# Dense experts of a two-layer decoder: products from coarse and fine operand parts, down products between up products

## The reference, cut to what matters

```
x_attn = _layernorm(x_flat, ln_g, ln_b) @ attn_w + attn_b + x_flat
g = x_attn.reshape(MICRO_BATCHES, E, tpe, Dx)           # 2 x 8 x 128 x 256
h = gelu(einsum('metd,edf->metf', g, w1) + b1)           # w1: 8 x 256 x 1024
y = einsum('metf,efd->metd', h, w2) + b2                 # w2: 8 x 1024 x 256
out = gelu(y @ next_w + next_b)                          # next_w: 256 x 256
x = _layernorm(x + out)                                  # the layer's end
```

## Time and profile before

| what | us |
|---|---|
| median of three runs (lowest, highest) | 2448.28 (2446.01, 2457.68) |
| span of the profiled execution | 2451.3 |
| PE busy | 2287.7 (93%) |
| DVE busy | 1509.6 (62%) |
| ACT busy | 1106.9 (45%) |
| POOL busy | 1062.9 (43%) |
| scatters (L353), 256: busy, and POOL's idle time before them | 416.9, 400.8 |
| first instruction of stage f, of stage d (PE) | 1569.28, 1741.41 |

### The profile page before, as it was taken

One profiled execution on the slowest core, in us unless ns is written; L12 is line 12 of the kernel. 1 busy time (PEld: TensorE's weight loads), 2 busy tenths in 40 slices (PEclk: granted clock), 3 DMA queues, 4 the chain that ended last, 5 costly groups with the idle time before them and its releaser, 6 DMA issues.

```text
span 2451.3 us, 34108 instructions
## 1 busy us (share of the span) xinstructions
PE 2287.7 (93%) x12918; PEld 1434.3 (59%) x12918; DVE 1509.6 (62%) x2293; ACT 1106.9 (45%) x2365; POOL 1062.9 (43%) x780
## 2 busy tenths in 40 slices
PE   6999999989988999999999999999899789979998
PEld 3333343367754555554655555787666657768887
DVE  6778678457744666665666676722344566565556
ACT  1567657733322444443344444332321467643323
POOL 2446546624443788884578786333301122100000
PEclk8899999999999999999999999999899899989999
DMA  6454333232110011112010111254300601020001
GB/s 127 120 98 87 73 68 74 64 90 48 1 18 1 11 15 15 15 28 44 1 15 11 15 15 20 78 159 103 86 2 25 154 24 45 1 65 14 1 1 35
DMA packets 137613, 114.21 MB, mean 47 GB/s; under 512 B 74501, under 2 KB 114931, under 8 KB 137065
## 3 DMA queue, kind: packets, MB, share of 16 engines
q1 hardware_dynamic: 100297, 111.08, 16.7%
q0 software_dynamic: 36864, 0.15, 4.3%
q10 hardware_dynamic: 288, 0.79, 0.2%
HBM read 85.99 MB, written 13.39 MB: 41 GB/s over the span
## 4 chain that ended last, share of the span: by engine, by line
PE 73%; DMA 11%; DVE 8%; ACT 4%; issue 2%; SPq 2%; POOL 0%; ACTq 0%; DVEq 0%; POOLq 0%
PE PS L128 70%; DMA adj<-e_EE,e_IX 8%; SPq L154 2%; PE PS L1248 1%; DVE a_MX L741 1%; DVE c_MX L1896 1%; ACT a_P L847 1%; DVE g_SS L132 1%; DMA a_KS<-a_KL 1%; DMA a_r<-a_RQ 1%; PE PS L360 1%; DVE c_AC L132 1%; DVE g_st L1339 0%; ACT g_SS L1433 0%; PE PS L361 0%
## 5 line engine op out<-in xcount | busy, mean ns | idle before, releaser
L353 POOL DMA_INDIRECT adj<-e_EE,e_IX x256 | 416.9, 1629 | 400.8 <-DMA adj<-e_EE,e_IX 345.9
L1896 DVE TENSOR_REDUCE c_MX<-PS 128x2 f32<-128x1024 f32 x256 | 313.0, 1222 | 176.2 <-PE PS L128 176.2
L132 POOL TENSOR_TENSOR c_AC<-c_AC,c_P 128x1024 f32<-128x1024 f32 x145 | 364.3, 2513 | 77.6 <-DVE c_AC L132 70.5
L1993 ACT ACTIVATE c_P<-PS 128x1024 f32<-128x1024 f32 x256 | 252.0, 1026 | 214.8 <-PE PS L128 214.8
L741 DVE TENSOR_REDUCE a_MX<-PS 128x2 f32<-128x1024 f32 x256 | 303.2, 1219 | 55.3 <-PE PS L128 54.2
L847 ACT ACTIVATE a_P<-PS 128x512 f32<-128x512 f32 x512 | 270.6, 601 | 87.2 <-PE PS L128 86.4
L128 PE MATMUL PS<-c_P,c_VV 128*64 128x512 f32 x1024 | 247.7, 605 | 0.0
L137 POOL TENSOR_SCALAR e_EQ<-e_KR,e_KC 128x128 bf16<-128x128 f32 x256 | 162.8, 636 | 159.4 <-DMA e_KR<-adj_key 121.5
L128 PE MATMUL PS<-a_QS,a_KS 64*128 64x512 f32 x512 | 194.3, 461 | 20.9 <-ACT a_P L847 8.8
L128 PEld LDWEIGHTS PS<-a_QS,a_KS 64*128 64x128 f32 x512 | 84.1, 189 | 172.2 <-ACT a_P L847 96.8
L128 PE MATMUL PS<-a_KS,a_QS 48*128 48x512 f32 x512 | 171.3, 477 | 10.0 <-DMA a_QS<-a_QH 4.8
(11 more groups left out here) (496 smaller groups left out, 4589.7 us busy)
## 6 DMA issues: line engine op xcount, KB each, us to landing
e_KR<-adj_key SPq DMA_DIRECT2D x64, 256.0 KB, 3.9
f_W<-in_L_ffn_w SPq DMA_DIRECT2D x16, 1024.0 KB, 7.5
c_RB<-c_r SPq DMA_DIRECT2D x58, 128.0 KB, 2.8
g_FB<-in_fside_1x16xSxS SPq DMA_DIRECT2D x8, 616.0 KB, 8.6
a_QS<-a_QH SPq DMA_DIRECT2D x32, 128.0 KB, 3.9
adj<-e_zt SPq DMA_DIRECT2D x16, 256.0 KB, 4.2
adj<-e_EE,e_IX POOLq DMA_INDIRECT x256, 3.2
d_AJ<-adj SPq DMA_DIRECT2D x8, 512.0 KB, 9.0
```

The lines of the kernel that those rows point to most:

```text
L132: return v.e.tensor_tensor(o, a, b, op)
L353: g.e.indirect_dma_start(self.adj, bass.IndirectOffsetOnAxis(ap=self.IXE[:, k:k + 1], axis=0), self.EE[:, k:k + 1], None, compute_op=ALU.a ...
L1896: v.e.reduce_max(MX[:, w % 2, :, qt, kh], bank(0, 2).rearrange("p (h n) -> p h n", h=2), AX, negate=True).then_inc(*smax_dve.up())
L1993: s.e.activation(PB[t % NP][:, :, :].rearrange("p h n -> p (h n)"), bank(2 + 2 * (t % 2), 2), ACT.Exp, scale=0.125).then_inc(*st_act.up())
```

## The change

All products of the expert part, and those with next_w, take their operands as a coarse part (the value rounded to fp32r, made by an ACT copy) plus a fine part (the value less its coarse part, made by a DVE subtraction). A product of two such operands is three products: coarse x coarse, fine x coarse, coarse x fine. ACT and DVE split GT as the turn part makes it (GH, GL), W1, W2 and next_w as they come (W1H, W1L ...; the fine part overwrites the loaded tensor, the coarse parts lie over tiles of stage d that are free), the hidden rows in pairs of blocks (HTH, HTL), and y (YTH, YTL). POOL has no part in it.

The expert part goes by pairs of blocks: step P makes the up products of pair P (2 blocks, 12 products) and then the down products of pair P-2 (12 products). The y sums have two pairs of banks in turn, o both halves in one bank, and its DVE and ACT work takes two tiles in one instruction. SP loads W1 of expert e after the up products of expert e-2, and W2 of it after the down products of expert e-2, each by itself. The transposes ("xt") of the first tiles come in steps 29 to 32.

```diff
-    GT = sb(c, "f_GT", [128, 2, 2048])
+    GH = sb(c, "f_GH", [128, 2, 2048], F32R)
+    GL = sb(c, "f_GL", [128, 2, 2048], F32R)
...
+    W1L = [K.over(f"f_W1L{i}", f"f_W1{i}", 0, [128, 2, 1024]) for i in range(2)]
+    W1H = [K.over(f"f_W1H{i}", "a_QH", 8192 * i, [128, 2, 1024]) for i in range(2)]
...
+            if i in (8, 12):
+                yield "split1", 0, i // 4 - 2
+            if i == 16:
+                yield "split_n",
+        for P in range(34):
+            e, p = divmod(P, 4)
+            if P < 32:
+                yield "h", P
+                if p < 2:
+                    yield "split2", e, p
+                elif e < 7:
+                    yield "split1", e + 1, p - 2
+            if P == 32:
+                yield "marks", 0
+            if P >= 2:
+                yield "y", P - 2
+            if P == 33:
+                yield "marks", 1
+            if p == 2 and e:
+                yield "o", e - 1
+            if P == 26:
                 yield "root", 0
-            for m in range(2):
-                yield "o", e, m
+            if 29 <= P < 33:
+                for n in range(3):
+                    yield "xt", 3 * (P - 29) + n
+        yield "o", 7
         yield "root", 1
...
             elif kind == "h":
-                e, f = a
...
-                for k in range(2):
-                    ins = mm(pe, bank(bk)[:, 0:256].rearrange("p (m t) -> p m t", m=2), W1[e % 2][:, k, 128 * f:128 * f + 128],
-                             gt_pair[k][:, :, 128 * e:128 * e + 128], k == 0, k == 1)
-                ins.then_inc(*h_pe.up())
+                pe.wait_ge(w1l_dve, 2 * e + p // 2 + 1)
+                pe.wait_ge(gl_dve, 16)
...
+                    parts = [(W, G, k) for k in range(2) for W, G in ((W1H, 0), (W1L, 0), (W1H, 1))]
+                    for q, (W, G, k) in enumerate(parts):
+                        ins = mm(pe, bank(n % 3)[:, 0:256].rearrange("p (m t) -> p m t", m=2),
+                                 W[e % 2][:, k, 128 * f:128 * f + 128], gt_pair[G][k][:, :, 128 * e:128 * e + 128], q == 0, q == 5)
+                    ins.then_inc(*h_pe.up())
             elif kind == "y":
...
+                pe.wait_ge(w2l_dve, 2 * e + p // 2 + 1)
+                pe.wait_ge(hl_dve, P + 1)
...
# DVE
+            elif kind == "turn_g":
+                t, = a
+                v.wait_ge(gt_act, t + 1)
+                tt(v, GL[:, :, t * 128:t * 128 + 128], halves(bank(6 + t % 2)[:, 0:256]),
+                   GH[:, :, t * 128:t * 128 + 128].bitcast(F32), ALU.subtract).then_inc(*gl_dve.up())
...
+            elif kind == "h":
+                P, = a
+                v.wait_ge(hh_act, P + 1)
+                tt(v, HTL[P % 4][:, :, :], HT[P % 4][:, :, :], HTH[P % 4][:, :, :].bitcast(F32),
+                   ALU.subtract).then_inc(*hl_dve.up())
...
# SP
         for e in range(8):
             if e > 1:
-                sp.wait_ge(y_pe, 2 * (e - 1))
+                sp.wait_ge(h_pe, 8 * (e - 1))
             dma(sp, W1[e % 2][:, :, :], A["L0_ffn_w1"][e].rearrange("(c p) n -> p c n", p=128)).then_inc(*w1_in[e % 2].up())
+            if e > 1:
+                sp.wait_ge(y_pe, 4 * (e - 1))
             dma(sp, W2[e % 2][:, :, :], A["L0_ffn_w2"][e].rearrange("(c p) n -> p c n", p=128)).then_inc(*w2_in[e % 2].up())
```

More of the change, by code:

```diff
@@ new lines, in tensor @@
+                e, p = divmod(P, 4)
+                pe.wait_ge(w1l_dve, 2 * e + p // 2 + 1)
+                pe.wait_ge(gl_dve, 16)
+                pe.wait_ge(cc_dve, 1)
+                for f in (2 * p, 2 * p + 1):
+                    n = 8 * e + f
+                    if n > 2:
+                        pe.wait_ge(h_act, n - 2)
+                    parts = [(W, G, k) for k in range(2) for W, G in ((W1H, 0), (W1L, 0), (W1H, 1))]
[3 more added lines that the diff above has]
+                    ins.then_inc(*h_pe.up())
+            elif kind == "y":
+                P, = a
+                e, p = divmod(P, 4)
+                pe.wait_ge(w2l_dve, 2 * e + p // 2 + 1)
+                pe.wait_ge(hl_dve, P + 1)
+                if e > 1:
+                    pe.wait_ge(yl_dve, 2 * (e - 1))
+                for d in range(2):
+                    parts = [(W, h, j) for j in range(2) for W, h in ((W2H, HTH), (W2L, HTH), (W2H, HTL))]
+                    for q, (W, h, j) in enumerate(parts):
+                        ins = mm(pe, bank(3 + d + 2 * (e % 2))[:, 0:256], W[e % 2][:, 2 * p + j, 128 * d:128 * d + 128],
+                                 h[P % 4][:, j, :], p == 0 and q == 0, p == 3 and q == 5)
@@ L2258, in tensor @@
                 ins.then_inc(*y_pe.up())
             elif kind == "o":
-                e, m = a
-                pe.wait_ge(y_dve, 2 * (e + 1))
-                pe.wait_ge(nw_in, 1)
+                e, = a
+                pe.wait_ge(yl_dve, 2 * (e + 1))
+                pe.wait_ge(nwl_dve, 1)
                 if e:
-                    pe.wait_ge(o_dve, 2 * e - 1 + m)
-                for k in range(2):
-                    ins = mm(pe, bank(5 + m)[:, 0:256], YT[e % 2][:, k, 128 * m:128 * m + 128], NW[:, k, :], k == 0, k == 1)
+                    pe.wait_ge(o_dve, e)
@@ L2267, in tensor @@
+                if e == 6:
+                    pe.wait_ge(xt_act, 3)
+                for m in range(2):
+                    parts = [(y, N, k) for k in range(2) for y, N in ((YTH, NWH), (YTH, NWL), (YTL, NWH))]
+                    for q, (y, N, k) in enumerate(parts):
+                        ins = mm(pe, bank(7)[:, 256 * m:256 * m + 256], y[e % 2][:, k, 128 * m:128 * m + 128], N[:, k, :],
+                                 q == 0, q == 5)
                 ins.then_inc(*o_pe.up())
@@ L2393, in scalar @@
             elif kind == "o":
-                e, m = a
-                i = e + 8 * m
-                s.wait_ge(o_dve, 2 * e + m + 1)
-                s.e.activation(TM[:, i % 4, :], TM[:, i % 4, :], ACT.Gelu).then_inc(*gelu_act.up())
+                e, = a
+                pair = TM[:, 2 * (e % 2):2 * (e % 2) + 2, :]
+                s.wait_ge(o_dve, e + 1)
+                s.e.activation(pair, pair, ACT.Gelu).then_inc(*gelu_act.up())
             elif kind == "root":
```

193 lines of the change are left out of this document (113 added, 80 removed).

## The result

The changed kernel took 2462.9 us, median of 9 runs (2451.4 to 2467.9); the kernel before, on the same chip, 2450.3 (9 runs, 2444.4 to 2457.8). The ratio is 1.0046, interval 1.0028 to 1.0063: 11 us slower. The forecast was 2450, and its range (given once as 2439 to 2459, once as 2438 to 2460) ended at 2460. So the change is a small loss, and the forecast of no change was wrong in time.

What follows compares the result with a forecast made beforehand. Stage f's scatter chain, delaying POOL's memsets, was taken as the bound. 0 (stage f, hidden) + 0 (loads) + 1 (descriptors) + 1 (clock) = +2 on 2451.3, with runs 3.0 below the profile: 2450 us, range 2439 to 2459 (also 2438 to 2460).

Steps and rivals of the forecast that it cites:

- the mechanism: Stage d's LB copies wait for POOL's memsets behind stage f's 44 scatters; about 12 us saved in stage f counts nothing.
- rival 2: Stage f's scatters slow by more than 12 us, from single loads or starved descriptors: 2460 to 2470 us; chance 0.05.
- Stage f alone: Stage f's own work, eight experts at 14 us plus tail, ends at 1729 us instead of 1741.
- the same tail of 11: End of stage f: last y, o, root and four transposes, some 11 us as before.
- the clock: After the longer wait for LB, PE restarts at 1.2 GHz: 1 us taken, bounds 0 and 3.
- rival 1: Expert part: PE falls to half clock and stage f becomes the bound, up to 2513 us; chance 0.08.
- the descriptors: POOL's descriptor writing for stage f's scatters slows beside a nearly full DVE: 1 us taken, bounds 0 and 7.6.
- the row of 1.75 us: Turn part: the scatter at 1589.00 us took 1.75 us on POOL instead of 1.55, sole evidence for slower descriptors.
- the sentence that the prediction leaned on: Skill's SBUF page: two-port DVE instructions keep POOL from writing descriptors, a tensor_tensor does not; used for stage f's scatters.
- the waits for landing: Stage f's scatters delayed beside twelve single loads instead of six pairs: 0 taken, bounds -13 and +13 us.

Runs made afterwards that it cites:

- send34 pair: The changed kernel and the kernel before, each with 34 instead of 44 scatters in stage f: ratios 0.9928 and 0.9973 to the kernel before.
- before_dve_red: Kernel before plus one DVE reduction of one SBUF operand behind each of the 64 up product groups: ratio 1.0000.
- before_dve_one: Kernel before plus one DVE multiplication of one SBUF operand by a scalar column behind each of the 64 up product groups: ratio 1.0011.

## Why the prediction was wrong

**Right: the mechanism.** The memsets of stage d stand behind 44 scatters, so a shorter stage f reaches nothing; the chain of waits stayed on the scatters; DVE's idle time before the LB copies (28.08 us) is put down to POOL. The send34 pair shows the hidden gain. What the forecast had wrong is the length of the chain that hides it: the memsets came 11.1 us later after the stage's start, where it allowed 10, and the scatters of more than 1.6 us are the sign that the prediction gave for rival 2.

**Nearly right: stage f alone.** 12 us shorter were forecast, 7.6 to 9.6 came. The first up product came 31.2 us after the stage's start (1587.7; 36.7 forecast, 30.7 at best). From there to stage d it was 133.4 us, which by the same tail of 11 is 15.3 per expert instead of 14; part of that is the gap at 1636 to 1641 us, where PE works 3.04 of 5 us and ACT's copy of W1 waits 3.7 us for its load. Copies and subtractions cost what stage h's rows gave: 1046 ns for 1042, 1224 for 1214, 688 for 687.

**Right: the clock.** It stood at 0.50 in the wait, and PE's 32 records after LB took 5.65 us instead of 5.44: 0.2 us, where I took 1. In the expert part the clock was 0.97, so rival 1 (half clock) is out.

**Wrong: the descriptors.** This is the step that failed. Of its bounds, 0 and 7.6 us, I took 1 "on the low side". It was 6.95 in the first profile and 8.1 in the second (76.94 - 68.88). The price lay at the upper bound although only 14 to 18 scatters, not 38, were longer: the row of 1.75 us was one hold of 0.2 us beside a 0.42 us instruction, and the new instructions are 1.23 us long, so that the excess of one scatter goes up to 1.03. I multiplied the excess of the row where I should have asked what it was a sample of. The trace of before has the answer, beside the scatter that starts at 1589.00 us:

```profile
1588.90 0.42 DVE L132 TENSOR_TENSOR f_TM<-f_TM,f_AB 128x256 f32<-128x256 f32 x1
```

It is a sum of two SBUF operands, and 0.32 us of it are left when the scatter starts; less 0.13 that is the excess of 0.20 within 0.01 us. So there was a row of before beside a tensor_tensor, which the prediction says is missing, and it spoke against the sentence that the prediction leaned on. Two more scatters of before were held, which I had not read: 1.75 us at 1578.87, beside a normalizing instruction of 0.41 us, and 1.64 at 1714.64, beside X<-X,f_TM of 0.43 us. An estimate from the durations: of starts that fall at random into an instruction of 1.23 us, half its length is left in the mean, less 0.13 us a hold of 0.49; the 14 held scatters were held 0.50 in the mean (6.95 us over 14). Rival 2, which had this price, got 0.05. By itself the step moves the forecast by 6 us, to 2456, still in its range; the measured time lies outside because the landing waits grew as well, and because the kernel before ran at 2450.3 us beside it, 2 us above the 2448.3 that the range was laid around.

The page that I leaned on says more than I weighed. The Trainium skill (SBUF — State Buffer, "Who interferes with whom") reports that tensor_tensor was not seen to stall a DMA, and marks its reason, that descriptor writing needs an interface which tensor_tensor leaves free, as inferred; that is the sentence I used. Two bullets above, the section says that a DVE instruction with two SBUF inputs contends with a GpSimd instruction that reads SBUF. The scatter has its indices and its values in SBUF (e_IX, e_EE). The trace agrees with that second sentence, with holds of up to 1.03 us, and not with the first. Its rule that tensor_reduce never contends agrees with before_dve_red (68.75 us), and that tensor_scalar can with before_dve_one (70.79).

**Wrong in size: the waits for landing.** I took 0 between -13 and +13, for the loads. The trace shows 4.9 us of longer landing waits in the changed kernel. That the single loads cause them is not shown: with the loads back in pairs the waits are as long (above). Their cause stays open.

So the sum should have read: 0 for stage f, 7 for holds, 5 for the waits, less 0.7 for the earlier first scatter, 0 for the clock: 11 us. Hiding the gain was forecast; that the hiding chain would be made longer by the very instructions that were added was not weighed as likely.

## What to carry to other kernels

When a chain of dependent scatters from GpSimd bounds a stage, every VectorE instruction that reads two SBUF operands, or runs at the doubled pace of a multiplication by a scalar column, is on that chain by the time it still has to run when a scatter starts: price it by its length, not by how busy VectorE is. Before work is moved to an engine that "has room", ask whose instructions it holds up. And where a gain is hidden behind another chain, change the length of that chain in the same step (here 34 scatters instead of 44): the changed kernel then goes from 0.5% slower to 0.7% faster, where the kernel before gains 0.3% by the same move.

## What the runs showed of the hardware

- A scatter that starts inside a DVE subtraction of two SBUF operands takes 1.55 us plus the rest of that instruction less 0.13 us; with two additions of two SBUF operands these are fourteen cases in the first profile, 0.07 to 1.03 us of excess. One scatter that started 0.03 us after such an instruction was not held (1653.44). A second subtraction behind the first does not hold it again: the scatter of 1642.97 was held 0.07 us by the end of the HTL subtraction, and not by the W1 subtraction of 1.23 us that starts at 1643.14.
- A reduction of the same length (1219 ns) holds nothing: 16 starts inside such runs, all 1.55 or 1.56 us.
- A multiplication of one SBUF operand by a scalar column takes 0.75 to 0.77 us for 1024 fp32 elements a partition, where a subtraction takes 1.22 to 1.23, and holds the scatter as well.
- The start of the same stage, behind the same unchanged code, lay between 1556.6 and 1572.7 us in fourteen profiles. It follows a long chain of scatters, so a single profile says nothing here of a total that differs by 10 us.
